# Half as many rests for GpSimd in the gather passes, each ended by a count of finished steps

## What is computed

```python
msg = e_w[:, None] * h[src]; agg = segment_sum(msg, dst)            # L0: three levels
msg = relu(concat([x[row], ef]) @ Wn1 + bn1) @ Wn2 + bn2            # L1: ef from edge attributes and times
out = segment_sum(msg, col) + x
xt = einsum("ni,rio->nro", x, W); agg = segment_sum(xt[src, etypes], dst)   # L2: two layers, 8 relations
a = einsum("ehd,ehd->eh", kT[src, :, etype], q[dst]) * pri / sqrt(d)        # L3: two layers, 32 relations
msg = m * edge_softmax(a, dst); hag = segment_sum(msg, dst)
```

## Time and profile before

| | |
|---|---|
| time, median of 3 runs | 6425.38 us (6423.44 to 6430.5) |
| the profiled execution's own time | 6410.16 us |
| its span (first to last instruction) | 6408.1 us |
| GpSimd busy | 3221.9 us, 50% of the span |
| TensorE busy | 3293.9 us, 51% |
| VectorE busy | 2162.9 us, 34% |
| ScalarE busy | 1006.4 us, 16% |
| gathers (line 479) | 3128, 3001.8 us busy, 960 ns of one |
| share of the 16 DMA engines, software queue | 16.2% |

### The profile page before, as it was taken

One profiled execution on the slowest core, in us unless ns is written; L12 is line 12 of the kernel. 1 busy time (PEld: TensorE's weight loads), 2 busy tenths in 40 slices (PEclk: granted clock), 3 DMA queues, 4 the chain that ended last, 5 costly groups with the idle time before them and its releaser, 6 DMA issues. The chain is left out here.

```text
span 6408.1 us, 51881 instructions
## 1 busy us (share of the span) xinstructions
PE 3293.9 (51%) x13857; PEld 2295.6 (36%) x13857; DVE 2162.9 (34%) x5075; ACT 1006.4 (16%) x2209; POOL 3221.9 (50%) x3406
## 2 busy tenths in 40 slices
PE   5554677767774555643463344643324356333263
PEld 3333455545552333332343232233324322333153
DVE  3222322232224222411121114533338544333485
ACT  0000322232222111200010002400004324000063
POOL 4665466546663666366646663046650320566403
PEclk7676777677776777755565556755557677555586
DMA  2111334333432332211131116976653579766453
GB/s 61 46 47 40 88 98 101 98 82 99 101 99 79 91 90 82 107 46 47 46 131 47 46 46 251 427 239 185 182 149 111 149 287 427 204 187 184 118 148 95
DMA packets 630965, 826.34 MB, mean 129 GB/s; under 512 B 93075, under 2 KB 510341, under 8 KB 618133
## 3 DMA queue, kind: packets, MB, share of 16 engines
q1 hardware_dynamic: 480117, 492.37, 22.9%
q0 software_dynamic: 120608, 276.12, 16.2%
q10 hardware_dynamic: 29952, 54.54, 2.9%
HBM read 470.63 MB, written 352.04 MB: 128 GB/s over the span
## 5 line engine op out<-in xcount | busy, mean ns | idle before, releaser
L479 POOL DMA_INDIRECT arena<-table,idx_s x3128 | 3001.8, 960 | 2353.5 <-issue 1095.5
L751 PE MATMUL ps<-arena,work 128*128 x4160 | 985.9, 378 | 1050.0 <-issue 934.9
L751 PEld LDWEIGHTS ps<-arena,work 128*128 128x128 f32 x4160 | 824.8, 274 | 1317.4 <-issue 1170.3
L1965 PE MATMUL ps<-arena,work 128*128 x1664 | 412.7, 426 | 693.7 <-issue 488.2
L1965 PEld LDWEIGHTS ps<-arena,work 128*128 128x128 f32 x1664 | 359.1, 317 | 748.6 <-issue 530.1
L459 DVE TENSOR_SCALAR work<-iota_row,dl_s,w_s 128x128 f32<-128x128 f32 x1248 | 350.4, 358 | 454.6 <-issue 349.4
L455 DVE TENSOR_TENSOR work<-ps,dl_s 128x512 f32<-128x512 f32 x208 | 143.8, 692 | 926.5 <-issue 617.0
L1934 DVE TENSOR_TENSOR arena<-arena,ps 128x128 f32<-128x128 f32 x832 | 182.7, 281 | 741.9 <-issue 500.0
L929 DVE SCALAR_TENSOR_TENSOR arena<-ps,vecs,arena 128x256 f32<-128x256 f32 x208 | 100.6, 484 | 893.9 <-issue 435.9
L1832 PE MATMUL ps<-arena,work 32*128 32x512 f32 x1600 | 299.1, 876 | 97.5 <-DVE work L1859 44.2
L510 PE MATMUL ps<-work,picks 128*104 128x512 f32 x416 | 313.4, 842 | 46.2 <-issue 42.8
(11 more groups left out here) (331 smaller groups left out, 3539.5 us busy)
## 6 DMA issues: line engine op xcount, KB each, us to landing
table<-arena SPq DMA_DIRECT2D x96, 2048.0 KB
onehot<-col_rows ACTq DMA_DIRECT2D x208, 256.0 KB
values<-arena SPq DMA_DIRECT2D x832, 64.0 KB
arena<-values SPq DMA_DIRECT2D x208, 256.0 KB
arena<-table,idx_s POOLq DMA_INDIRECT x3128
arena<-edge_times SPq DMA_DIRECT2D x208, 128.0 KB
edge_part<-arena SPq DMA_DIRECT2D x208, 128.0 KB
table<-arena SPq DMA_DIRECT2D x50, 512.0 KB
```

Source lines behind the costliest of these rows:

```text
L479: pool.indirect_dma_start(ring[:, ds(t % RING * 2 * H, width)], None, tab, bass.IndirectOffsetOnAxis(ap=idx_s[:, t:t + 1], axis=0)).then_i ...
L751: mm = pe.matmul(accf[:, ds(b, P)], o, arena[:, ds(slot, H)], start=False, stop=False, skip_group_check=True)
L1965: mm = pe.matmul(ps[:, n % 8, c * P:(c + 1) * P], across_ring[:, n % DEEP, c * P:(c + 1) * P], Qn_flat[:, ds(b, P)], start=True, stop=True)
```

## The change

The number of quads between rests doubles: 8 instead of 4, and 4 instead of 2 in the passes with an edge share. That makes 120 rests of 240. What ends a rest changes too. After GpSimd has handed over the quad that has just landed, it also waits until the steps of all quads but that last one are reported done: by `quad_done` (TensorE) in passes 1 to 6 and by `mixed` (VectorE) in the score passes. How many step quads that are depends on the destinations, so the setup makes a table of 24 counts, `done_i`: its entry r is the number of step quads whose `need_i` is at most 4r+3. GpSimd reads its entry into a register before it waits for the landing.

```diff
+RESTS = 24
+        done_i = sb("done_i", [P, RESTS], I32)
+        rested = signal("rested")
+        need_f, rest_f = arena[:, 16000:16000 + ALL_QUADS], arena[:, 16200:16200 + RESTS]
+        met = arena[:, 16300:16300 + RESTS * ALL_QUADS].rearrange("p (r n) -> p r n", r=RESTS)
...
                 ch(dve.tensor_scalar(need_i[:, :], need_i[:, :], 2, None, ALU.arith_shift_right))
+                ch(dve.tensor_copy(need_f, need_i[:, :]))
+                ch(dve.tensor_scalar(rest_f, jrow[:, 0:RESTS], 4.0, 3.0, ALU.mult, ALU.add))
+                ch(dve.tensor_tensor(met, need_f.unsqueeze(1).to_broadcast([P, RESTS, ALL_QUADS]),
+                                     rest_f.unsqueeze(2).to_broadcast([P, RESTS, ALL_QUADS]), ALU.is_le))
+                ch(dve.tensor_reduce(rest_f, met, AX.X, ALU.add))
+                ch(dve.tensor_copy(done_i[:, :], rest_f))
...
-        def gathers(pool, tab, width, freed, joins=None, rest=4):
+        def gathers(pool, tab, width, freed, done, joins=None, rest=8):
...
                 pool.sem_inc(arrived.sem, 1)
+                handed[0] = k + 1
...
                 if t % 4 == 3:
-                    done = t // 4 + 1
-                    for k in range(handed[0], done if done % rest == 0 else done - 1):
-                        hand_over(k)
-                        handed[0] = k + 1
+                    k = t // 4
+                    if handed[0] < k:
+                        hand_over(k - 1)
+                    if k % rest == rest - 1:
+                        if done is None:
+                            hand_over(k)
+                            continue
+                        used = pool.value_load(done_i[0:1, k // 4:k // 4 + 1], min_val=1, max_val=ALL_QUADS)
+                        hand_over(k)
+                        pool.wait_ge(done.sem, used + done.base)
+                        pool.sem_inc(rested.sem, 1)
...
-                    gathers(pool, tab, H, freed, rest=2 if edges else 4)
+                    gathers(pool, tab, H, freed, quad_done, rest=4 if edges else 8)
...
-                    gathers(pool, table, H, freed, joins, rest=4)
+                    gathers(pool, table, H, freed, quad_done, joins, rest=8)
...
-                        gathers(pool, table32, 2 * H, freed, rest=4)
+                        gathers(pool, table32, 2 * H, freed, mixed, rest=8)
```

## The result

In the first comparison the changed kernel took 6896.18 us (median of 4 runs, 6878.71 to 7140.76) against 6424.41 us for the kernel before (4 runs, 6408.07 to 6430.5): 1.073 of before, interval 1.071 to 1.076. One of the four, 7140.76 us, had a granted clock of 0.527 in place of 0.636 and is not in the ratio. Forecast were 6256 us. So the change made the kernel 472 us slower, where I had said 169 us faster.

A forecast was written before the change was run, and what follows sets the result against it. GpSimd's issue rate and rests were taken to bound all eight gather passes. -281 + 90 + 60 + 5 + 5 - 35 - 13 = -169 us from 6410.16 gives 6241, plus 15 carried over 6256 us; range 6180 to 6330.

The forecast's parts named there:

- What bounds the kernel: In all eight gather passes GpSimd's issue rate, 1.25 us a gather, and its rests set the length.
- the rests taken out: 120 rests go: 96 in passes 1 to 6 at 2.1 us, 24 in the score passes at 3.3; 281 us gained.
- The kept rests of passes 2 and 3: 48 rests stay; 10 of them lengthened by 6 us because TensorE is behind: 60 us lost, bounds 0 and 322.
- The kept rests of the others: Passes 1, 5 and 6: 36 rests stay, half lengthened by 5 us as TensorE is behind: 90 us, at most 360.
- the spells: Stretches in passes 1, 5 and 6 where TensorE's half products come singly, 2.1 or 2.8 us apart, and it falls behind.
- Passes 4, 7 and 8: 36 rests stay at 0 to 1 us each; with table reading and semaphore instructions in all 120 rests, 5 us.
- Slot stops: GpSimd's waits between rests for slots TensorE hasn't freed, passes 1, 5, 6; with stretched rests 35 us, all to go.
- The tails: TensorE's lateness at the ends of passes 1, 5 and 6: some 9 us stay, 13 us less over the three.
- The setup: Five added VectorE instructions before the gather passes cost 5 us, bounds 4 and 7.
- The 2.15 us: Pass 1 rests: a DMA rule, about 2.0 us plus bytes over 436 GB/s, was said to agree with the trace.
- The slower one: GpSimd waits for a late TensorE at three quarters of 84 kept rests, passes 1, 2, 3, 5, 6: 6558 us; chance 0.14.
- Spells only when instructions are recorded: TensorE's slow stretches exist only under recording, so timed runs lack their costs and gains: 6154 us; chance 0.15.

The follow-up runs named there:

- chip 12: A later set on another chip: the changed kernel and the kernel before, both unchanged, at 6091.51 against 6350.74 us, ratio 0.959.
- the quiet chips: Chips 12, 6 and 5 of three later sets, with the changed kernel against the kernel before, both unchanged: ratios 0.959, 0.958 and 0.959.

## Why the prediction was wrong

**What bounds the kernel, and the rests taken out: right.** In every pass GpSimd's rate and its rests set the length, and taking rests out is paid in full. On chip 12, from one trace to the other, passes 1 to 6 are 193 us shorter (202 expected) and passes 7 and 8 79 us (79 expected). The versions with fewer and fewer rests, down to none, follow 2.1 and 3.3 us a rest all the way on the quiet chips: 240 rests x these is 192 x 2.1 + 48 x 3.3 = 562 us, measured 576.

**The kept rests of passes 2 and 3: the step that failed.** I took 10 of 48 rests at 6 us, 60 us. In the first comparison all 48 were long (7.3 to 16.2 us), 48 x (11.4 - 2.4) = 430 us, above even my upper bound of 322. That bound supposed 1.5 step quads left over and 2.7 us to a hold-up's end. The timeline of pass 2 shows what came in its place: the three computing engines are idle for 7.5 to 11.4 us each, 6.4 us of it together, and the chain of one step quad (TensorE, ScalarE, VectorE, TensorE) starts again only when the gathers have stopped. What holds it up isn't known.

**The kept rests of the others.** Passes 1, 5 and 6: 90 us expected, 12 x (8.4 + 6.6 + 6.6 - 3 x 2.4) = 173 us measured. Here the mechanism was another one too. By the stricter count the spells of the changed kernel are 134, 21 and 26 us in passes 1, 5 and 6, against 214, 230 and 121 before, so in passes 5 and 6 they are mostly gone. The rests are 6.6 us all the same, and in half of them the work was done and only its report late, which the prediction doesn't have at all. Its last sentence named what would refute it, long rests in passes 2 and 3 as a rule, and that came. Passes 4, 7 and 8 are the worse mistake of kind: I costed them at 5 us for all, as their consumers had never been late. Pass 4's rests are 8.6 us, 12 x (8.55 - 2.45) = 73 us in all, and passes 7 and 8 are 21 and 20 us longer where 39 us less was expected each. Not having been late with a rest every 20 us was no evidence for a rest every 40 us. I had written that against myself for passes 2 and 3, in the rival, and not applied it here.

**The small terms: right.** Slot stops of passes 1, 5 and 6 are gone. The tails went from 17.7, 10.3 and 9.9 us to 5.1, 5.8 and 5.7, 21 us where I said 13. The setup is 5.6 us longer at the first gather (69.6 against 64.0) where I said 5 (6.9 to 8.2 us on the quiet chips, the larger ones over the bound of 7); of the new instructions the two large ones take

```profile
36.35 2.76 DVE L423 TENSOR_TENSOR arena<-arena 128x2496 f32<-128x2496 f32 x1
39.14 2.75 DVE L425 TENSOR_REDUCE arena<-arena 128x24 f32<-128x2496 f32 x1
```

2.7 us each was the estimate. The 2.15 us that the prediction sets beside pass 1 as in agreement are 0.26 us under the mean rest there, 2.41 us.

**On the quiet chips** the gain of 257 to 261 us is the 281 us of the rests less some 20 for the setup and the new ending. The 150 us that I charged for long rests and the 48 us that I credited for stops and tails aren't there, so the forecast of 169 us is too small for the same step: it took the spells for a property of the kernel.

**The account of the first comparison.** -281 (rests) + 430 + 173 + 73 (kept rests of passes 1 to 6) - 35 (slots) + (21 + 20 + 79 = 120, what passes 7 and 8 lost on top of their expected gain) is 480 us against 453 measured over the passes. With 6 in the setup, 21 less in tails and 43 more until the last value stores of passes 7 and 8, the 453 become 481 of the 493 us between the two spans.

**The rivals.** The slower one, spells soon after each rest, has the right sign and was given 0.14. TensorE is late at the kept rests as it says, but in passes 5 and 6 not through spells; it expected 6558 us, three quarters of 84 rests at 6.7 to 7.8 us, and is short by 338 us through passes 2 and 3 (9 us a rest) and the three passes it left out. "Spells only when instructions are recorded" gave 6154 us, ratio 0.958, and the quiet chips have 0.958 to 0.959, since there the spells are indeed absent. That the number fits is luck, since the rival's reason doesn't hold alone: the quiet traces are recordings too, with 2.6 times as many updates, and have no spells. Whether recording had a part in the first session is not shown: each timed run of every set has a span and a granted clock of its own, so they seem to be recorded too, and no run here was surely without recording. For such a part speaks that the first comparison's traces lack 6 in 10 semaphore updates. The rival's steps of 0.7 us in SyncE's register work are real and belong to that session as well: between SyncE's 3424 instructions 573 intervals are 0.7, 1.4, 2.1 or 2.8 us to within 0.02 in the first trace of the kernel before, and 23 on chip 12; VectorE has 24 and 13. The Trainium skill (NOTIFIC — the notification-queue block, 7.1) states that the block's inner pipeline holds producers back rather than lose a record, while a full ring may drop new ones. Complete instruction records together with stalled engines and missing updates would fit both halves; no run here shows the block at work.

**What stays open.** Why the engines and their reports were held up in the first comparison and not in the other four sets. The two traces of that session show it, all 8 executions there were slower than any of the same kernel later, and none of the traces that followed has it. It lasted through one session on one chip of unknown number, so it may belong to that chip or to that time, and the recording may be its cause or may suffer with the engines. I couldn't bring it about. How the versions without the count wait do under it was not seen either: they wait for TensorE only when the ring is full, and the kernel before, which does the same, lost 1.3% there (6424 against 6341 us; of 60 us between its spans there and on chip 12, 35 lie in the gather passes). That they would lose as little is an inference, since its rests are also closer together.

## What to carry to other kernels

A rest that ends with another engine's count is only as short as that engine's slowest report. Those that ended with the transfer's own landing stayed at means of 2.4 to 2.6 us in passes 1 to 6 of the kernel before, in the very session in which the others grew to 6.6 to 11.4 us. If a first comparison contradicts an account that adds up in all other terms, run the same two kernels again on another chip before explaining the difference by the program, and compare the number of recorded semaphore updates: where it differs for the same program, as 36,908 and 99,000 here, the two traces come from different conditions. And when taking half of something out pays in full, try taking out all of it.

## What the runs showed of the hardware that I had not expected

- 391 gathers in a row, 488.3 us without a pause, cost no more each than those between rests (369.4 us busy in pass 1, against 370.2), in pass 4 some 6 us more (400.0 against 394.2). With 77% of the DMA engines' time in use in the score passes, the longest idle time between two gathers was 1.2 us, put down to a landing: no stop for one of the 60 slots shows.
- In one session TensorE, VectorE and ScalarE were idle together for over 5 and up to 10.2 us, 34 times in passes 2 and 3 of the changed kernel, most of it while GpSimd issued indirect DMAs. In the rest shown ScalarE went on 0.2 us behind the last one's end. On chip 12 the same instructions have no such stretch over 3.8 us.
- Reports came late as well: in 12 rests of passes 5 and 6 GpSimd's wait ended 6.0 to 6.8 us after the step quad that it asked for, where on chip 12 a report stands 0.01 us behind its quad.
- The kernel before is 1.3% slower in that session and the changed one 13%. They differ in the spacing of the rests and in what ends them. The releasers of the long rests point at the wait for the count, but no version with only one of the two changes ran in that session.
